# A two-layer perceiver on one core: the serial stretches cut in halves and spread over more engines

## The reference, cut to what matters

```python
xm = x * time_mix + x_m1 * (1.0 - time_mix) + x_comb * combined_mix
k = jnp.exp(jnp.minimum(xm @ Wk.T, 60.0)); v = xm @ Wv.T; r = xm @ Wr.T
# _wkv, one step per row
no = jnp.maximum(p, u + kt); e1 = jnp.exp(p - no); e2 = jnp.exp(u + kt - no)
y = (e1 * a + e2 * vt) / (e1 * bb + e2)
no2 = jnp.maximum(w + p, kt); e1 = jnp.exp(w + p - no2); e2 = jnp.exp(kt - no2)
a, bb, p = e1 * a + e2 * vt, e1 * bb + e2, no2
# then (sigmoid(r) * wkv) @ Wo.T, a residual, and the feed-forward:
h = bit_linear(x, w1)                 # 1024 columns; inputs rounded to 255 steps per row, ternary weights
h = silu(depthwise_conv1d(h.T, conv_w, conv_b).T)       # three taps along the rows
return bit_linear(h, w2)
```

## Time and profile before

| | us |
|---|---|
| three timed runs | 1058.40, 1062.74, 1066.01 |
| median | 1062.74 |
| profiled execution, its own time | 1060.48 |
| its span in the trace | 1058.70 |
| layer 0 blocks, then the rest of layer 0 | about 37 to 503, 503 to 553 |
| layer 1 blocks, then the tail | about 564 to 1009, 1009 to 1058.7 |

### The profile page before, as it was taken

One profiled execution on the slowest core, in us unless ns is written; L12 is line 12 of the kernel. 1 busy time (PEld: TensorE's weight loads), 2 busy tenths in 40 slices (PEclk: granted clock), 3 DMA queues, 4 the chain that ended last, 5 costly groups with the idle time before them and its releaser, 6 DMA issues. The chain is left out here.

```text
span 1058.7 us, 30772 instructions
## 1 busy us (share of the span) xinstructions
PE 1006.5 (95%) x12909; PEld 683.0 (65%) x12909; DVE 737.1 (70%) x1726; ACT 678.1 (64%) x956; POOL 421.2 (40%) x376
## 2 busy tenths in 40 slices
PE   8899999999999999998877899999999999999977
PEld 5466666666666666665554566667676666666665
DVE  4788888888888888876448766665565565566465
ACT  3577778787787877876543555665656566555722
POOL 4269888888888888881000000010100101000000
PEclk9899999999999999999999999999999999999998
DMA  8411122012220122113022010111100111000000
GB/s 315 141 31 46 68 72 72 23 51 72 72 72 19 54 72 71 54 40 120 11 94 95 2 37 2 37 37 36 37 21 18 37 37 37 2 2 2 2 1 5
DMA packets 14681, 53.31 MB, mean 50 GB/s; under 512 B 3024, under 2 KB 4816, under 8 KB 13648
## 3 DMA queue, kind: packets, MB, share of 16 engines
q1 hardware_dynamic: 14544, 51.35, 13.8%
HBM read 51.21 MB, written 0.13 MB: 48 GB/s over the span
## 5 line engine op out<-in xcount | busy, mean ns | idle before, releaser
L793 DVE TENSOR_REDUCE tile_max<-ps_max 128x1 f32<-128x448 f32 x346 | 204.5, 619 | 147.7 <-PE ps_max L1112 143.7
L790 DVE CUSTOM_DVE_ANT_0 unread<-ps_max,masks 128x448 bf16<-128x448 f32 x372 | 218.3, 621 | 71.9 <-PE ps_max L1112 71.7
L462 POOL TENSOR_TENSOR probs<-probs,masks 128x512 f32<-128x512 f32 x182 | 227.9, 1274 | 70.0 <-ACT probs L576 68.5
L588 ACT ACTIVATE probs<-ps_scores 128x1024 f32<-128x1024 f32 x193 | 187.2, 1021 | 88.2 <-PE ps_scores L1166 88.0
L583 ACT ACTIVATE probs<-probs 128x1024 f32<-128x1024 f32 x196 | 207.3, 1057 | 53.0 <-DVE probs L850 44.2
L1166 PE MATMUL ps_scores<-q_pad,k_full 32*128 32x256 f32 x3088 | 232.2, 376 | 0.0
L1184 PE MATMUL ps_out<-probs,values 128*32 128x128 f32 x6272 | 215.2, 277 | 0.7 <-ACT probs L588 0.4
L1166 PEld LDWEIGHTS ps_scores<-q_pad,k_full 32*128 32x128 f32 x3088 | 193.2, 186 | 0.8
L1184 PEld LDWEIGHTS ps_out<-probs,values 128*32 128x32 f32 x6272 | 159.6, 110 | 51.5 <-issue 47.5
L1112 PE MATMUL ps_max<-k_high,q_high 32*128 32x448 bf16 x722 | 171.9, 359 | 7.9 <-DVE tile_max L793 4.9
L1105 PE MATMUL ps_proj<-ctx_t,wk 128*128 128x448 f32 x384 | 171.0, 568 | 1.7
(11 more groups left out here) (254 smaller groups left out, 924.8 us busy)
## 6 DMA issues: line engine op xcount, KB each, us to landing
ctx_t<-in_ctx_t SPq DMA_DIRECT2D x28, 896.0 KB, 5.2
masks<-in_mask_n SPq DMA_DIRECT2D x14, 448.0 KB, 3.4
masks<-in_mask_t SPq DMA_DIRECT2D x14, 448.0 KB, 3.4
room_w<-in_L_attn_f_w SPq DMA_DIRECT2D x2, 1024.0 KB, 7.2
room_w<-in_L_ffn_w SPq DMA_DIRECT2D x2, 1024.0 KB, 8.5
room_w<-in_L_ffn_w_gate SPq DMA_DIRECT2D x1, 1024.0 KB, 10.6
room_w<-in_L_ffn_w_up SPq DMA_DIRECT2D x1, 1024.0 KB, 13.0
room_w<-in_L_ffn_w_down SPq DMA_DIRECT2D x1, 1024.0 KB, 14.9
```

The costliest lines, as they stand in the source:

```text
L462: nc.gpsimd.tensor_tensor(p, p, three(mask_t[m % 2], TILES)[:, t, :].unsqueeze(1).to_broadcast([P, 4, P]), ALU.add).then_inc(sig("bias_add ...
L588: nc.scalar.activation(prob(T, half), scores_half(T, half), ACT.Exp).then_inc(sig(f"exp_done{half}"), 1)
L790: ins = v.tensor_tensor_reduce(unread[:, j % 2, :], max_bank(m, j)[:, 0:HALF], mask_n[m % 2][:, HALF * half:HALF * (half + 1)], 1.0, -3e38 ...
L793: ins = v.tensor_reduce(tile_max[:, h, half:half + 1], max_bank(m, j)[:, 0:HALF], AX_X, ALU.max)
```

## The change

- The block starts: `acc` is cleared before the maxima, and the turned rows are copied before the decay. In block 13 the sums are copied before the exponentials.
- Both quantisations of 1024 columns run as two halves of 512 (`quant_halves`), as do the turning, the copy and the hidden tile in front of the convolution.
- GpSimd adds `first_t` to the keys, forms the numerator into `uk`, and makes all three taps of chunk 7.
- ScalarE makes the first product of the mixed rows for chunk 1, takes the four exponentials in two goes, and asks for the SiLU table early.
- VectorE's `x4` sum stands behind small constants; fillers on TensorE go from 3 to 1, 18 to 13, 11 to 8, 8 to 1 and 5, and 2 to none.

The diff, without context and indentation:

```diff
@@ -305,0 +310,4 @@
+  CONV_SPLIT = tuple(range(FC - 1))
+  CONV_DONE = (FC // 2, len(CONV_SPLIT))
@@ -508,0 +517,25 @@
+  pool.wait_ge(sig("mix_made"), 3)
+  pool.wait_ge(sig("k_exp"), 1)
+  for c in range(DC):
+      nc.gpsimd.tensor_scalar(three(uk)[:, c, :], three(kk)[:, c, :], first_t[:, c:c + 1], None, ALU.add).then_inc(sig("first_added"), 1)
+  pool.wait_ge(sig("exps"), 2)
+  pool.wait_ge(sig("aa_ready"), DC)
+  nc.gpsimd.tensor_tensor(three(uk), three(aa)[:, :, 0:P], ee[:, 0:D].rearrange("p (c t) -> p c t", c=DC), ALU.mult).then_inc(sig("numerator"), 1)
+  pool.wait_ge(sig("numerator"), 1)
+  pool.wait_ge(sig("ev_ready"), 1)
+  nc.gpsimd.tensor_tensor(uk, uk, ev, ALU.add).then_inc(sig("numerator"), 1)
+  pool.wait_ge(sig("hidden_ready"), 2)
+  for c in range(len(CONV_SPLIT), FC):
+      nc.gpsimd.tensor_scalar(hc[:, c, :], hp[:, c, 1:P + 1], conv_w[:, c, 1:2], conv_b[:, c:c + 1], ALU.mult, ALU.add).then_inc(sig("pool_conv"), 1)
+  done = FC - len(CONV_SPLIT)
+  for k in (0, 2):
+      for c in range(len(CONV_SPLIT), FC):
+          tap = nc.gpsimd.tensor_scalar(xn[:, 0:P], hp[:, c, k:P + k], conv_w[:, c, k:k + 1], None, ALU.mult)
+          tap.then_inc(sig("pool_conv"), 1)
+          pool.wait_ge(sig("pool_conv"), done + 1)
+          nc.gpsimd.tensor_tensor(hc[:, c, :], hc[:, c, :], xn[:, 0:P], ALU.add).then_inc(sig("pool_conv"), 1)
+          pool.wait_ge(sig("pool_conv"), done + 2)
+          done += 2
+  def lent_out(m, t):
+      if not (m == NB - 1 and t == 0):
+          stage_sums(m, t)
@@ -636 +672,0 @@
-  max_out(NB * l)
@@ -637,0 +674 @@
+  max_out(NB * l)
@@ -642,0 +680,2 @@
+  if t == 0:
+      stage_sums(m, t)
@@ -697,2 +736,3 @@
-  act.wait_ge(sig("hq_turned"), 1)
-  nc.scalar.copy(bigt.bitcast(BF16), ps_max[:, 0, :].bitcast(BF16)).then_inc(sig("hq_ready"), 1)
+  for half in range(2):
+      act.wait_ge(sig("hq_turned"), half + 1)
+      nc.scalar.copy(bigt.bitcast(BF16)[:, 512 * half:512 * (half + 1)], hidden_bank(half)).then_inc(sig("hq_ready"), 1)
@@ -704,0 +745,2 @@
+  act.wait_ge(sig("turned_copied"), 7)
+  nc.scalar.activation(three(xm)[:, 1, :], three(rt)[:, 1, 1:P + 1], ACT.Identity, scale=t_mix[:, 1:2]).then_inc(sig("xm_begun"), 1)
@@ -709,2 +751,3 @@
-  act.wait_ge(sig("exponents"), 1)
-  nc.scalar.activation(ee, dd, ACT.Exp).then_inc(sig("exps"), 1)
+  for first in (2 * D, 0):
+      act.wait_ge(sig("exponents"), 1 + int(first == 0))
+      nc.scalar.activation(ee[:, first:first + 2 * D], dd[:, first:first + 2 * D], ACT.Exp).then_inc(sig("exps"), 1)
@@ -712,0 +756,2 @@
+  act.wait_ge(sig("table_loaded"), 3)
+  nc.scalar.activation(stat[:, 30:31], ones[:, 0:1], ACT.Silu).then_inc(sig("table_loaded"), 1)
@@ -715,3 +760,2 @@
-  act.wait_ge(sig("hidden_ready"), 1)
-  for c in range(FC):
+  for c in CONV_SPLIT:
+      act.wait_ge(sig("hidden_ready"), c // 4 + 1)
@@ -721 +765,3 @@
-  act.wait_ge(sig("conv_done"), FC // 2 * (g + 1))
+  act.wait_ge(sig("conv_done"), CONV_DONE[g])
+  if g == 1 and len(CONV_SPLIT) < FC:
+      act.wait_ge(sig("pool_conv"), 5 * (FC - len(CONV_SPLIT)))
@@ -724,2 +770,3 @@
-  act.wait_ge(sig("sq_turned"), 1)
-  nc.scalar.copy(hqt, ps_max[:, 1, :].bitcast(BF16)).then_inc(sig("sq_ready"), 1)
+  for half in range(2):
+      act.wait_ge(sig("sq_turned"), half + 1)
+      nc.scalar.copy(hqt[:, 512 * half:512 * (half + 1)], ps_max[:, half, :].bitcast(BF16)[:, 0:512]).then_inc(sig("sq_ready"), 1)
...
+  def quant_halves(src, dst, w, at, arrived, name):
+      for half in range(2):
+          arrived(half)
+          note(v.tensor_reduce(stat[:, 12 + 16 * half:13 + 16 * half], src(half), AX_X, ALU.max, apply_absolute_value=True))
+      dve.wait_ge(sig("dve_link"), links[0])
+      link(v.tensor_scalar(stat[:, 13:14], stat[:, 12:13], stat[:, 28:29], 1e-5, ALU.max, ALU.max))
+      link(v.reciprocal(stat[:, 14:15], stat[:, 13:14]))
+      link(v.tensor_scalar(stat[:, 15:16], stat[:, 14:15], 127.0, None, ALU.mult))
+      for half in range(2):
+          cols = slice(512 * half, 512 * (half + 1))
+          rounded(src(half), tmp_big(FF)[:, cols], dst[:, cols]).then_inc(sig(name), 1)
+      note(v.tensor_scalar(stat[:, at:at + 1], stat[:, 13:14], 1.0 / 127.0, w_inv[:, w:w + 1], ALU.mult, ALU.mult))
+      dve.wait_ge(sig("dve_link"), links[0])
@@ -885,0 +953 @@
+  v.memset(acc[:, :, :], 0.0)
@@ -894 +961,0 @@
-  link(v.memset(acc[:, :, :], 0.0))
...
-  dve.wait_ge(sig("dve_link"), links[0])
-  out_(quant(big, FF, bigq.bitcast(BF16), (2,), 22), "hq_made")
+  quant_halves(lambda half: big[:, 512 * half:512 * (half + 1)], bigq.bitcast(BF16), 2, 22, gated, "hq_made")
...
@@ -988,3 +1054,0 @@
-  dve.wait_ge(sig("wo_ready"), 1)
-  link(v.tensor_tensor(x4, ps_proj[:, 0:D], x4, ALU.add))
...
+  dve.wait_ge(sig("wo_ready"), 1)
+  link(v.tensor_tensor(x4, ps_proj[:, 0:D], x4, ALU.add))
@@ -1004 +1071,4 @@
-  link(v.tensor_scalar(xm3[:, c, :], now, t_mix[:, c:c + 1], None, ALU.mult))
+  if c == 0:
+      link(v.tensor_scalar(xm3[:, c, :], now, t_mix[:, c:c + 1], None, ALU.mult))
+  else:
+      dve.wait_ge(sig("xm_begun"), 1)
@@ -1013,3 +1083 @@
-  v.tensor_tensor_scan(pm3[:, c, 1:P + 1], decay_t[:, c:c + 1].to_broadcast([P, P]), kk3[:, c, :], -1e38, ALU.add, ALU.max)
-  link(v.tensor_scalar(uk3[:, c, :], kk3[:, c, :], first_t[:, c:c + 1], None, ALU.add))
+  note(v.tensor_tensor_scan(pm3[:, c, 1:P + 1], decay_t[:, c:c + 1].to_broadcast([P, P]), kk3[:, c, :], -1e38, ALU.add, ALU.max))
@@ -1018,3 +1086 @@
-  link(v.tensor_tensor(three(den), pm3[:, :, 0:P], uk3, ALU.max))
-  v.tensor_tensor(d4[:, 0], pm3[:, :, 0:P], three(den), ALU.subtract)
-  v.tensor_tensor(d4[:, 1], uk3, three(den), ALU.subtract)
+  dve.wait_ge(sig("dve_link"), links[0])
@@ -1024 +1090,5 @@
-  out_(v.tensor_tensor(d4[:, 3], kk3, pm3[:, :, 1:P + 1], ALU.subtract), "exponents")
+  v.tensor_tensor(d4[:, 3], kk3, pm3[:, :, 1:P + 1], ALU.subtract).then_inc(sig("exponents"), 1)
+  dve.wait_ge(sig("first_added"), DC)
+  link(v.tensor_tensor(three(den), pm3[:, :, 0:P], uk3, ALU.max))
+  v.tensor_tensor(d4[:, 0], pm3[:, :, 0:P], three(den), ALU.subtract)
+  v.tensor_tensor(d4[:, 1], uk3, three(den), ALU.subtract).then_inc(sig("exponents"), 1)
@@ -1031,5 +1101,8 @@
-      v.tensor_tensor_scan(three(aa)[:, c, 1:P + 1], e4[:, 2, c], three(ev)[:, c, :], 0.0, ALU.mult, ALU.add)
-      link(v.tensor_tensor_scan(three(bb)[:, c, 1:P + 1], e4[:, 2, c], e4[:, 3, c], 0.0, ALU.mult, ALU.add))
-  note(v.tensor_tensor(three(den), three(bb)[:, :, 0:P], e4[:, 0], ALU.mult))
-  link(v.tensor_tensor(three(ev), vps, e4[:, 1], ALU.mult))
+      v.tensor_tensor_scan(three(aa)[:, c, 1:P + 1], e4[:, 2, c], three(ev)[:, c, :], 0.0, ALU.mult, ALU.add).then_inc(sig("aa_ready"), 1)
+  for c in range(DC):
+      note(v.tensor_tensor_scan(three(bb)[:, c, 1:P + 1], e4[:, 2, c], e4[:, 3, c], 0.0, ALU.mult, ALU.add))
+  dve.wait_ge(sig("dve_link"), links[0])
+  dve.wait_ge(sig("exps"), 2)
+  dve.wait_ge(sig("aa_ready"), DC)
+  v.tensor_tensor(three(ev), vps, e4[:, 1], ALU.mult).then_inc(sig("ev_ready"), 1)
+  link(v.tensor_tensor(three(den), three(bb)[:, :, 0:P], e4[:, 0], ALU.mult))
@@ -1038 +1110,0 @@
-  note(v.tensor_tensor(three(num), three(aa)[:, :, 0:P], e4[:, 0], ALU.mult))
@@ -1040,2 +1112,2 @@
-  link(v.tensor_tensor(num, num, ev, ALU.add))
-  out_(v.tensor_tensor(num, num, den, ALU.mult), "wkv_ready")
+  dve.wait_ge(sig("numerator"), 2)
+  out_(v.tensor_tensor(num, uk, den, ALU.mult), "wkv_ready")
@@ -1051,14 +1123,19 @@
...
+  for half in range(2):
+      dve.wait_ge(sig("w1_ready"), half + 1)
+      v.tensor_tensor(hp[:, 4 * half:4 * half + 4, 1:P + 1], ps_scores[:, half, :].rearrange("p (c t) -> p c t", t=P),
+                      step_row.unsqueeze(1).to_broadcast([P, 4, P]), ALU.mult).then_inc(sig("hidden_ready"), 1)
+  dve.wait_ge(sig("hidden_ready"), 2)
+  for chunks in (CONV_SPLIT[0:FC // 2], CONV_SPLIT[FC // 2:]):
+      for c in chunks:
+          dve.wait_ge(sig("conv_first"), c + 1)
+          v.scalar_tensor_tensor(out=hc[:, c, :], in0=hp[:, c, 0:P], scalar=conv_w[:, c, 0:1], in1=hc[:, c, :],
+                                 op0=ALU.mult, op1=ALU.add).then_inc(sig("conv_mid"), 1)
+      for c in chunks:
+          dve.wait_ge(sig("conv_mid"), c + 1)
+          v.scalar_tensor_tensor(out=hc[:, c, :], in0=hp[:, c, 2:P + 2], scalar=conv_w[:, c, 2:3], in1=hc[:, c, :],
+                                 op0=ALU.mult, op1=ALU.add).then_inc(sig("conv_done"), 1)
+  def turned_back(half):
+      dve.wait_ge(sig("hs_turned"), half + 1)
+  quant_halves(lambda half: ps_scores[:, 2 + half, :], hq, 4, 26, turned_back, "sq_made")
...
-  pe.wait_ge(sig("hq_ready"), 1)
+  for half in range(2):
+      pe.wait_ge(sig("hq_made"), half + 1)
+      for c in range(4):
+          at = 512 * half + P * c
+          last = tr(hidden_bank(half)[:, P * c:P * (c + 1)], xq[:, at:at + P], ident16[:, :])
+      last.then_inc(sig("hq_turned"), 1)
@@ -1401,0 +1479 @@
+  pe.wait_ge(sig("hq_ready"), c // 4 + 1)
@@ -1407 +1485 @@
-  idle_products(3)
+  idle_products(1)
```

(27 more changed lines are left out.)

43 lines of the change are left out of this document (14 added, 29 removed).

## The result

| | median us (range, runs) | TensorE at its low clock, mean us | at equal clock |
|---|---|---|---|
| before | 1061.84 (1058.28 to 1066.01, 6); the later runs alone 1061.37 (62) | 24.9 | 1061.5 ± 0.1 |
| changed | 1053.59 (1049.37 to 1056.83, 6); these and the later runs 1052.67 (12) | 26.1 | 1052.2 ± 0.2 |

A forecast was written before the change was run, and what follows sets the result against it. TensorE was taken to bound the block loops and an engine-to-engine chain the tail. Eight terms, 0.8 + 0.3 + 1.3 + 0.75 + 0.75 + 2.6 + 3.7 + 0.4 = 10.6, off 1061.9 gave 1051.3 us, range 1046.5 to 1056.5.

The forecast's parts named there:

- Term 6: Recurrence: key sums leave VectorE, the e3 product's wait goes, two passes move to GpSimd; 2.6 us saved, least 1.7.
- Term 7: Convolution to the end: halves start engines earlier, fewer VectorE taps, shorter last half, fillers no longer late; 3.7 us, least 2.2.
- Terms 1 to 3: First block start 0.8 us, second block start 0.3, block 13's sums copied before the exponentials 1.3.
- only the tail pays: Rival: gains at block starts and block 13 end as later waits, so 2.4 us go; 1053.7 us, 18%.
- Term 4: Gated feed-forward: quantising in halves leaves only a half to turn, copy and multiply last; 0.75 us saved, low case 0.2.
- Term 5: Start of the tail: two fillers fewer, constants moved into a wait, one product to ScalarE; 0.75 us, least 0.5.
- two passes leave it, 0.46 each: 0.9: Recurrence: aa by e0 and the sum with the values leave VectorE's list for GpSimd, saving 0.9 us.
- 1.0 earlier: Convolution: the hidden tile's first half reaches ScalarE after 512 columns instead of 1024, 1.0 us earlier.
- VectorE makes 14 taps instead of 16: Convolution: with fewer taps and no wait for all, part of the second SiLU starting about 2.05 us earlier.
- Term 8: TensorE's clock: the low clock may fall before, in or behind the tail's projection; 0.4 us saved, range -0.9 to 0.9.
- GpSimd is late: Rival: GpSimd runs slower beside VectorE and delays convolution by 1.6 us and recurrence by 1.0; 1053.9 us, 20%.

The follow-up runs named there:

- experiment 2: Changed kernel with the earlier kernel's filler counts (3, 18, 11, and 2 in the gated feed-forward): 1050.52 us, ratio 0.9887 to the kernel before.
- experiment 10: Changed kernel, GpSimd's product held to the reciprocal, no GpSimd in convolution, 18 fillers, plus one filler in each of two waits before the tail: 1050.24 us, 0.9902.
- experiment 12: The kernel of experiment 10 with four more fillers at the end of the tail: 1049.37 us, ratio 0.9904 to the kernel before.
- experiment 7: Changed kernel with GpSimd's product of aa with e0 held back until VectorE begins the reciprocal: 1051.14 us, ratio 0.9902 to the kernel before.
- experiment 4: Changed kernel with all eight convolution chunks on ScalarE and VectorE, none on GpSimd: 1051.43 us, ratio 0.9894 to the kernel before.
- experiment 1: The kernel before, unedited, run again to get each run's granted clock: 1061.76 us, ratio 0.9992.
- experiment 11: Changed kernel with two convolution chunks on GpSimd instead of one: one profiled execution, 1051.62 us.
- experiment 6: Kernel before with only the block edits (rows copied first, acc cleared early, block 13 sums first): 1056.01 us, ratio 0.9947.

## Why the prediction came out as it did

The forecast was 10.6; 9.3 ± 0.3 was there at equal clock, and the first median showed 8.2. The sign, the range and most mechanisms held. Part of the closeness is luck: terms 6 and 7 together brought 1.6 less than forecast, while the blocks and a part that I cannot place brought 1.0 more.

- *Terms 1 to 3 (2.4)*: right as a sum, which no run splits; 3.0 added to the kernel before, 2.8 taken from the changed one. The rival "only the tail pays" falls.
- *Term 4 (0.75)*: 0.44 (8.54 to 8.10). VectorE's last rounding ended 0.66 later from the first gated product on, where the term had 0.37; what follows was 1.10 shorter, as put (1.14). And its reason was incomplete. I costed the halves and passed over the two fillers that went; experiment 2 shows that the halves' gain exists only because they went.
- *Term 5 (0.75)*: right where the clock allows. From acc to the first scan 11.57 before and 10.79 in experiments 10 and 12, 0.78 less; in the profile after it was 12.98, since the low clock lay on it. That price was not in the term.
- *Term 6 (2.6)*: 1.8 (10.84 to 9.08). The wait for the exponentials went as put (1.55 for 1.7). The failing step is "two passes leave it, 0.46 each: 0.9": 0.2 came. I priced what leaves VectorE's list and checked whether GpSimd would be in time, but held VectorE's other passes at their old lengths. They grew by 0.75; moved beside the reciprocal, GpSimd gives the 0.96 in full (6.31 to 5.35).
- *Term 7 (3.7)*: 2.9, of which the table shows 2.5: 1.14 from the hidden tile to the second maximum and 1.35 behind it, where about 1.8 was put. The other 0.45 lies ahead of the hidden tile. TensorE's products for it and VectorE's first multiplication, before and then after:

```profile
1038.67 1.07 PE L1439 MATMUL ps_scores<-xn_t,tern 128*128 128x128 bf16 x16 [0.35 <-ACT xn_t L714]
1039.85 1.22 DVE L1052 TENSOR_TENSOR masks<-ps_scores,probs 128x1024 f32<-128x1024 f32 x1 [1.13 <-PE ps_scores L1439]
```
```profile
1037.92 1.07 PE L1517 MATMUL ps_scores<-xn_t,tern 128*128 128x128 bf16 x16 [0.35 <-ACT xn_t L759]
1038.65 1.29 DVE L1125 TENSOR_TENSOR masks<-ps_scores,probs 128x512 f32<-128x512 f32 x2 [0.68 <-PE ps_scores L1517]
```

The multiplication starts 0.73 behind the first product instead of 1.18. In this profile fillers at the low clock had held up the turn ahead of it by 0.5, so the step still reads 6.27; in experiments 7, 10 and 12 it is 5.82. ScalarE's first tap comes 0.73 behind the multiplication's start instead of 1.26, so the "1.0 earlier" was right for ScalarE. VectorE must still multiply the second half, and its own taps start only 0.55 earlier behind the hidden tile (1.32 in experiment 4, 1.87 in experiment 1). From the first product on, the second SiLU came 1.6 earlier instead of 2.05. The failing step is "VectorE makes 14 taps instead of 16": it gave nothing, for the same reason (0.5). From the hidden tile to the last sum it took 13.8, where the prediction named 12.5 as its sign; it had put the whole term there, also what lies ahead of the hidden tile.

- *Term 8 (0.4)*: nothing came on the average (24.9 us low before, 26.1 after). Which way each place falls shows in the profiles: with 13 fillers the projection before x5 took 2.07 us in 6 of 7, with 18 in 2 of 7 (1.13 in the others). These are single profiles of many versions, and among the three of them with the whole tail of the kernel before, two were low as well. If the difference holds, the shorter fillers give away about 0.9 us in half of the executions, which was in no term; it is a hint, not shown.

The parts sum to 2.9 + 0.4 + 0.8 + 1.8 + 2.9 = 8.8; 0.5 of the 9.3 is not placed, within the errors of these parts together. The rival "GpSimd is late" was wrong as written: it never was. Its ground was right. The Trainium skill ("GPSIMD Engine Reference", "Key points") says that both engines contend when VectorE has two SBUF inputs, and the trace agrees: such passes grew, the reciprocal did not. I had taken the rule to slow GpSimd; here it was mostly VectorE that paid. GpSimd's two-input passes did not grow; of its one-input passes (L535) the one that ran with VectorE idle, in experiment 11, took 0.60, the others there 0.70 to 0.71.

What stays open is where the clock falls. In all ten profiles of versions with block or tail edits and unfilled waits, the low clock came on or just ahead of the tail's first projection; in both with filled waits and in both of the kernel before it did not. Views by stretches of experiment 1's kernel and of experiment 6's show the same TensorE work before it (us, PE, PEld, DVE, ACT, POOL busy, PEclk, DMA):

```profile
1006.00:1007.00 1.00, 0.63 (x4) 0.42 (x4) 1.00 (x2) 0.00 (x0) 0.00 (x0) 1.00 0.00 0
1007.00:1008.00 1.00, 0.65 (x3) 0.60 (x4) 0.93 (x3) 0.00 (x0) 0.00 (x0) 1.00 0.00 0
```
```profile
1001.10:1002.10 1.00, 0.63 (x4) 0.40 (x4) 1.00 (x2) 0.00 (x0) 0.00 (x0) 1.00 0.00 0
1002.10:1003.10 1.00, 0.67 (x2) 0.58 (x3) 0.93 (x3) 0.00 (x0) 0.00 (x0) 0.67 0.00 0
```

Filling the waits kept it away twice in two; what makes the same lull fall in one kernel and not in the other, these runs do not tell.

## What to carry to other kernels

Before moving elementwise work to GpSimd, price not only its own time but what stands on VectorE meanwhile: beside passes that read two SBUF tiles the move may return next to nothing, beside a one-input pass such as a reciprocal it returned all (0.96 of 0.92). A list cut in halves gains only up to the next engine's own list, and only if no filler stands in front of the freed half. Compare kernels whose TensorE clock wanders at equal clock, by regressing time on low-clock time over the runs of each, and read one profile by its steps; but look at the raw means too, since equal clock leaves out what an edit does to the clock itself.

## What the runs showed of the hardware

- VectorE beside GpSimd: two scans of sums over 128 columns 0.71 to 1.15 us, a product over 256 columns 0.42 to 0.74, four taps with two SBUF inputs over 128 columns 1.14 to 1.40. In each of these groups of several passes one pass took most of the growth (0.40 to 0.83, 0.35 to 0.57). The reciprocal stayed at 1.75.
- GpSimd took 0.63 to 0.68 for two inputs over 256 columns, beside such passes or beside the reciprocal, and 0.45 to 0.46 over 128, beside VectorE's taps or with VectorE idle (experiment 11).
- One us more at TensorE's low clock goes with 0.32 us more time on the average.
